# Order of work inside the last attention: head turning split in pairs around each projection, and the queries' projection one group earlier

## The reference, cut to what matters

```python
q = rms_norm(linear(x, q_w, q_b), norm_q_w).reshape(B, L, NH, HD)          # NH = 16 heads of HD = 32
k = rms_norm(linear(ctx_txt, k_w, k_b), norm_k_w).reshape(B, -1, NH, HD)    # text rows 257 to 360
v = linear(ctx_txt, v_w, v_b).reshape(B, -1, NH, HD)
k_img = rms_norm(linear(ctx_img, k_img_w, k_img_b), norm_k_img_w)...        # image rows 0 to 256
v_img = linear(ctx_img, v_img_w, v_img_b)...
img_x = attention(q, k_img, v_img)                                          # softmax over 257 rows
txt_x = attention(q, k, v)                                                  # softmax over 104 rows
out = (txt_x + img_x).reshape(B, L, DIM)
return linear(out, o_w, o_b)
```

## Time and profile before

| what | value |
|---|---|
| three executions | 2484.36, 2490.7, 2493.62 us; median 2490.7 us |
| span of the profiled execution | 2493.3 us |
| TensorE (PE) busy in the span | 2377.4 us, 95% |
| VectorE (DVE), ScalarE (ACT), GpSimd (POOL) busy | 54%, 32%, 29% |
| mean granted TensorE clock | 0.959 of full speed |
| last attention, from its first matmul to the next stage's | about 1936 to 2334 us |

### The profile page before, as it was taken

One profiled execution on the slowest core, in us unless ns is written; L12 is line 12 of the kernel. 1 busy time (PEld: TensorE's weight loads), 2 busy tenths in 40 slices (PEclk: granted clock), 3 DMA queues, 4 the chain that ended last, 5 costly groups with the idle time before them and its releaser, 6 DMA issues. The chain is left out here.

```text
span 2493.3 us, 30147 instructions
## 1 busy us (share of the span) xinstructions
PE 2377.4 (95%) x10329; PEld 1284.9 (52%) x10329; DVE 1345.9 (54%) x3448; ACT 786.8 (32%) x2069; POOL 733.4 (29%) x728
## 2 busy tenths in 40 slices
PE   8999999989999998999979999989999899999899
PEld 4455455656356555555555565544444344444454
DVE  5544344126111324667667767676664355555797
ACT  1134344303011113555541010231110255655433
POOL 3655455204100004321133433320000165665200
PEclk9999999999999998999959999889999899999799
DMA  6026200014275533110043222450000321111100
GB/s 193 1 80 227 79 17 8 0 52 135 89 286 207 202 133 87 49 38 30 1 154 129 92 76 101 164 195 6 4 9 5 110 59 46 55 47 29 37 13 15
DMA packets 93678, 203.31 MB, mean 82 GB/s; under 512 B 18580, under 2 KB 37428, under 8 KB 91864
## 3 DMA queue, kind: packets, MB, share of 16 engines
q1 hardware_dynamic: 87384, 188.26, 22.4%
q0 software_dynamic: 6144, 13.13, 1.9%
HBM read 150.45 MB, written 45.94 MB: 79 GB/s over the span
## 5 line engine op out<-in xcount | busy, mean ns | idle before, releaser
L3645 POOL TENSOR_SCALAR a_p<-a_p,a_li 100x257 f32<-100x257 f32 x252 | 188.0, 766 | 110.7 <-DVE a_li L3508 110.7
L633 POOL TENSOR_SCALAR a_shared<-a_shared,a_li 128x361 f32<-128x361 f32 x104 | 131.5, 1265 | 182.7 <-DVE a_li L541 182.7
L3263 PE MATMUL bank<-l_early,a_ctx 128*128 128x512 f32 (+1 forms) x384 | 180.1, 614 | 0.0
L2560 PE MATMUL bank<-s_xT,s_w 128*128 128x400 f32 x512 | 179.2, 504 | 0.8 <-PEq L2757 0.8
L2560 PEld LDWEIGHTS bank<-s_xT,s_w 128*128 128x128 f32 x512 | 98.2, 192 | 77.2 <-issue 4.1
L1853 POOL DMA_INDIRECT a_got<-slots_y,slots_of x32 | 33.7, 1054 | 318.6 <-POOLq L1193 309.8
L3263 PEld LDWEIGHTS bank<-l_early,a_ctx 128*128 128x128 f32 (+1 forms) x384 | 68.8, 188 | 85.0 <-issue 85.0
L313 PE MATMUL bank<-a_wk,a_ctx 128*128 128x512 f32 (+1 forms) x192 | 95.0, 616 | 9.3 <-DMA a_wk<-in_L_xattn_Wk 5.6
L691 ACT ACTIVATE a_shared<-a_shared,a_nm 128x361 f32<-128x361 f32 x104 | 62.1, 597 | 98.9 <-DVE a_nm L535 98.9
L2570 PE MATMUL bank<-f_h,s_w 128*128 128x400 f32 x256 | 90.9, 499 | 0.0
L2629 ACT ACTIVATE f_sg<-bank 128x400 f32<-128x400 f32 x32 | 16.1, 503 | 236.6 <-PE bank L2560 236.6
(11 more groups left out here) (477 smaller groups left out, 4985.1 us busy)
## 6 DMA issues: line engine op xcount, KB each, us to landing
slots_x<-zero SPq DMA_DIRECT2D x4, 4096.0 KB, 27.0
f_triple<-in_L_ffn_triples SPq DMA_DIRECT2D x16, 768.0 KB, 4.3
rounded<-f_triple SPq DMA_DIRECT2D x16, 768.0 KB, 3.3
s_whole<-in_L_ffn_w SPq DMA_DIRECT2D x24, 512.0 KB, 3.9
e_wg<-in_L_ffn_w_gate SPq DMA_DIRECT2D x16, 704.0 KB, 4.5
e_wu<-in_L_ffn_w_up SPq DMA_DIRECT2D x16, 704.0 KB, 6.1
e_wd<-in_L_ffn_w_down SPq DMA_DIRECT2D x16, 512.0 KB, 4.4
e_xg<-slots_x SPq DMA_DIRECT2D x16, 512.0 KB, 5.4
```

Source lines behind the costliest of these rows:

```text
L633: pool.tensor_scalar(p[s % NP], p[s % NP], li[:, b % 2, h:h + 1], None, ALU.mult).then_inc(normed, 1)
L2560: mm = nc.tensor.matmul(banks[f % 2][:, 0:GT], w[:, kc, f * P:(f + 1) * P], xT[:, kc, :], start=(kc == 0), stop=(kc == KC - 1))
L3263: mm = nc.tensor.matmul(bank[0:m, :], columns[:, kc], w[:, kc, :], start=(kc == 0), stop=(kc == KC - 1))
L3645: pool.tensor_scalar(p[g % 2][j][:, lo:hi], p[g % 2][j][:, lo:hi], li[:, h, i:i + 1], None, ALU.mult) \
```

## The change

In every pass of the loop (b = 0 to 6) each group now reads: scores, two heads turned, a product, two heads turned, the rest. `queries(n)` moves from the third group to the second; `values(n, 0)` from the second to the third; `values(n, 1)` goes behind `turn_keys` and `turn_queries`, which now come before `outputs(b, 2)`; `values(n, 2)` goes from before `scores(n, 0)` to behind them. The ring's list follows. On VectorE `copy_heads` is cut in pairs, the key scaling and `add_query_bias` move ahead of the third group's maxima, and in the last group the maxima and inverses of the next sequence's first group come before copies. On GpSimd `key_power` comes before `norm(b, 2)` instead of after it. ScalarE's order of squares, signs and copies follows.

```diff
@@ order of the ring
-            for g in range(G):
-                if more:
-                    order += [[("k", n, 0)], [("k", n, 2)], [("q", n)], [("v", n, 2)]][g]
-                elif g == 0:
-                    order += [("o", b - 1)]
-                order += [("t", b, GH * g + j) for j in range(GH)]
-                if more:
-                    order += [[("x", n), ("k", n, 1)], [("v", n, 0)],
-                              [("v", n, 1)] + [("kT", n, fb) for fb in range(KC)] + [("qT", n)], []][g]
-                if b > 0 and more and g == 3:
-                    order += [("o", b - 1)]
+            two = lambda g, i: [("t", b, GH * g + 2 * i + j) for j in range(2)]
+            if more:
+                order += two(0, 0) + [("k", n, 0)] + two(0, 1) + [("x", n), ("k", n, 1)]
+                order += two(1, 0) + [("k", n, 2)] + two(1, 1) + [("q", n)]
+                order += two(2, 0) + [("v", n, 0)] + two(2, 1) + [("kT", n, fb) for fb in range(KC)] + [("qT", n), ("v", n, 1)]
+                order += two(3, 0) + [("v", n, 2)] + two(3, 1) + ([("o", b - 1)] if b > 0 else [])
+            else:
+                order += [("o", b - 1)] + [("t", b, h) for h in range(NH)]
@@ TensorE
                     scores(b, 1)
+                    turn_heads(b, 0, (0, 1))
                     keys(n, 0)
-                    turn_heads(b, 0)
+                    turn_heads(b, 0, (2, 3))
                     turn_x(n)
                     keys(n, 1)
                     outputs(b, 0)
 
                     scores(b, 2)
+                    turn_heads(b, 1, (0, 1))
                     keys(n, 2)
-                    turn_heads(b, 1)
+                    turn_heads(b, 1, (2, 3))
+                    queries(n)
+                    outputs(b, 1)
+
+                    scores(b, 3)
+                    turn_heads(b, 2, (0, 1))
                     values(n, 0)
-                    outputs(b, 1)
-
-                    scores(b, 3)
-                    queries(n)
-                    turn_heads(b, 2)
+                    turn_heads(b, 2, (2, 3))
+                    turn_keys(n)
+                    turn_queries(n)
                     values(n, 1)
                     outputs(b, 2)
-                    turn_keys(n)
-                    turn_queries(n)
+
+                    scores(n, 0)
+                    turn_heads(b, 3, (0, 1))
                     values(n, 2)
-
-                    scores(n, 0)
-                    turn_heads(b, 3)
+                    turn_heads(b, 3, (2, 3))
                     if b > 0:
                         project_out(b - 1)
                     outputs(b, 3)
@@ VectorE
                     all_maxima(b, 1)
+                    copy_heads(b, 0, (0, 1))
                     add_bias(n, 0)
-                    copy_heads(b, 0)
+                    copy_heads(b, 0, (2, 3))
                     inverses(b, 1)
                     add_bias(n, 1)
 
                     all_maxima(b, 2)
+                    copy_heads(b, 1, (0, 1))
                     add_bias(n, 2)
-                    copy_heads(b, 1)
+                    lay_last_key(n)
+                    copy_heads(b, 1, (2, 3))
                     inverses(b, 2)
-                    lay_last_key(n)
+                    mean_key_squares(n)
                     if b + 2 < B:
                         measure(b + 2)
+                    scale_keys(n)
+                    add_query_bias(n)
 
                     all_maxima(b, 3)
-                    mean_key_squares(n)
-                    add_query_bias(n)
-                    copy_heads(b, 2)
+                    copy_heads(b, 2, (0, 1))
                     mean_query_squares(n)
-                    inverses(b, 3)
-                    scale_keys(n)
+                    copy_heads(b, 2, (2, 3))
                     scale_queries(n)
                     copy_keys(n)
-
-                    copy_heads(b, 3)
+                    inverses(b, 3)
+
                     all_maxima(n, 0)
+                    copy_heads(b, 3, (0, 1))
+                    inverses(n, 0)
+                    copy_heads(b, 3, (2, 3))
                     if b > 0:
                         add_output(b - 1)
-                    inverses(n, 0)
@@ GpSimd
                     norm(b, 1)
                     if b + 1 < B:
                         add_bias(b + 1)
+                        key_power(b + 1)
                     norm(b, 2)
                     if b + 1 < B:
-                        key_power(b + 1)
                         query_power(b + 1)
@@ ScalarE
                     exponentials(b, 2)
+                    squares(n, 2)
                     signs(b, 1)
-                    squares(n, 2)
+                    query_squares(n)
+
+                    exponentials(b, 3)
                     copy_values(n, 0)
-
-                    exponentials(b, 3)
-                    query_squares(n)
+                    copy_keys(n)
                     copy_values(n, 1)
-                    copy_keys(n)
-                    copy_values(n, 2)
                     if n == B - 1:
                         signs(b, 2)
+
                     exponentials(n, 0)
+                    copy_values(n, 2)
```

More of the change, by code:

```diff
@@ L3324, in scores, with turn_heads @@
                             .then_inc(scored, 1)
-                def turn_heads(b, g):
-                    for j in range(GH):
+                def turn_heads(b, g, heads=range(GH)):
+                    for j in heads:
                         h = GH * g + j
@@ L3389, in _ @@
                     scores(b, 2)
+                    turn_heads(b, 1, (0, 1))
                     keys(n, 2)
-                    turn_heads(b, 1)
-                    values(n, 0)
+                    turn_heads(b, 1, (2, 3))
+                    queries(n)
                     outputs(b, 1)
                     scores(b, 3)
-                    queries(n)
-                    turn_heads(b, 2)
+                    turn_heads(b, 2, (0, 1))
+                    values(n, 0)
+                    turn_heads(b, 2, (2, 3))
+                    turn_keys(n)
+                    turn_queries(n)
                     values(n, 1)
                     outputs(b, 2)
-                    turn_keys(n)
-                    turn_queries(n)
+                    scores(n, 0)
+                    turn_heads(b, 3, (0, 1))
                     values(n, 2)
-                    scores(n, 0)
-                    turn_heads(b, 3)
+                    turn_heads(b, 3, (2, 3))
                     if b > 0:
@@ L3530, in all_maxima, with copy_heads @@
                         maxima(b, g, j)
-                def copy_heads(b, g):
-                    for j in range(GH):
+                def copy_heads(b, g, heads=range(GH)):
+                    for j in heads:
                         copy_head(b, g, j)
```

## The result

| | before | after |
|---|---|---|
| median of the runs | 2490.86 us (5 runs) | 2475.31 us (5 runs, 2465.33 to 2476.90) |
| span of the profiled execution | 2493.3 us | 2466.6 us |
| last attention, first matmul to next stage | 398.43 us | 383.61 us |

The ratio is 0.993, 95% interval 0.991 to 0.9949: the change makes the kernel faster by 0.7%. I had forecast 0.9975 and "within 0.5%". The median lies just inside my range (2475 to 2495), on its lower edge, but the move, 0.7%, is nearly three times the 0.25% that I gave.

What follows compares the result with a forecast made beforehand. TensorE was taken to bound the kernel; steady passes -0.8, seam -2.5 and clock -3.0 us sum to -6.3, a span of 2487.0 us and a median of 2484.4 (ratio 0.9975), range 2475 to 2495 us.

Steps and rivals of the forecast that it cites:

- The place of the work: Last attention: TensorE sets the pace, work only moves, so a steady sequence can win only what TensorE loses in waits.
- the price list of the steady pass: TensorE's queue laid out step by step: remaining waits 1.45 us against 1.56, a sequence 44.12 us, -0.11.
- the 0.55 us wait that I put before `turn_queries`: Third group: `turn_queries` waits 0.55 us for VectorE's copy of the second key block, behind head copy and query scaling.
- The price of a pair of heads: Each group: six transpositions, two heads, priced at 0.76 us, half of 1.51.
- The clean price of a head: Kernel before: twelve transpositions with nothing in their way take 1.51 us, the measure for other groups' losses.
- the floor: Steady sequence at full clock without the counted waits: 44.23 - 1.56 = 42.67 us.
- all gone is -1.56: Bound for a steady sequence: with all six predicted waits gone, -1.56 us, or -10.9 us over seven passes.
- rival 1: The steady waits really go: 1.0 us a sequence won, -12.5 us in all, 2478 us; chance 0.20.
- The wait for `norm(b, 2)`: Third group's second head waits 0.40 us, as `norm(b, 2)` behind `key_power` starts 8.5 us after `scores(b, 2)`.
- The seam: Where sequence 0 gives way to 1: 11.56 us falls to 8.3, gain 3.2 us, net -2.5 us.
- The clock: Sequence 1: the low clock behind the idle stretch, costing a product 3.0 us more, no longer occurs: -3.0 us.
- rivals 2 and 4: Seam gains but clock still falls there: 2487.5 us, chance 0.12; clock falls in each sequence: 2505 us, chance 0.04.

Runs made afterwards that it cites:

- scores_forward: Changed kernel with the next group's scores before the bank-waiting step in groups 0, 1, 3, and `key_power` behind `norm(b, 2)`: steady pass 41.56 us, ratio 0.989.
- seam_only: Kernel before with the new order in the first pass (b = 0) only: seven passes 309.8 us against 316.9, ratio 0.9978.
- steady_only: Kernel before with the new order in passes b = 1 to 6 only: seven passes 309.7 us against 316.9, ratio 0.9978.
- root_behind_norm: Changed kernel with `key_power` put back behind `norm(b, 2)` on GpSimd: steady pass 49.4 to 51.1 us, ratio 1.0145 against the kernel before.
- inverses_early: Kernel before with `inverses(n, 0)` moved ahead of `add_output(b - 1)` on VectorE: steady pass 43.7 us against 44.23, ratio 0.9988.
- four_in_a_run: Changed kernel with pairs undone, each group turning four heads in one run behind its product: steady pass 44.6 us, ratio 0.9989 against the kernel before.

## Why the prediction was wrong

**The place of the work** was right: TensorE sets the pace, the product count is the same, and the gain lies in TensorE's waits, its clock and, for a smaller part that I hadn't foreseen, in shorter products. By starts, the 1.33 us of a steady pass are 0.77 in the turning of heads, 0.37 in the products and 0.19 before `scores(b, 1)`.

**The step that failed is the price list of the steady pass.** I gave a pass -0.11 us and it gained 1.33. The largest term of the miss is the 0.55 us wait that I put before `turn_queries`, and which isn't there (0.59 with what the turning itself took less). The price of a pair of heads was too high by more than the bank waits behind it were too low, which makes 0.28, and that of a product was too high, 0.29. Another 0.11 is a slip of the sum: my own prices and waits add up to 44.01 us, and I wrote 44.12. The rest, outputs and scores, is 0.05 the other way.

**The clean price of a head** came from the first step, the floor. I wrote that "a run of twelve transpositions with nothing in their way takes 1.51 us (2159.01 to 2160.52)". It had something in its way. TensorE's weight loads in the kernel before at that place:

```profile
2159.01 0.85 PEld L3336 LDWEIGHTS bank<-ident,a_p 100*128 100x128 f32 x9 [0.53 <-issue]
2160.11 0.32 PEld L3336 LDWEIGHTS bank<-ident,a_p 100*128 100x128 f32 x3 [0.26 <-issue]
```

Nine loads, three heads, in 0.85 us, and then a gap before the fourth head. VectorE in the kernel before at that time:

```profile
2159.53 1.60 DVE L3513 COPY a_pt<-bank 128x300 f32<-128x300 f32 x4 [4.60 <-PE bank L3336]
```

The first of these copies lasts 0.47 us, so the first head's bank is free at 2160.0, and the fourth head, three places later in a ring of three banks, starts at 2160.11. `norm` of that group had ended at 2155.98, so it isn't that. The timeline of the matmuls hides this, since their modelled ends reach over the gap, and no idle time is written. Nine loads of 0.15 us each in 0.85 start 0.087 apart. A pair of heads with its neighbours is 0.59 us in the changed kernel, and two more heads at that distance add 0.52, so I estimate a run of four without any wait at 1.11 and not 1.51. The third group's run in the kernel before, which I had not read from its starts:

```profile
2146.69 0.69 PE L3336 MATMUL bank<-ident,a_p 100*128 100x100 f32 x6
...
2148.46 3.70 PE L3263 MATMUL bank<-l_early,a_ctx 128*128 128x512 f32 x8
```

It takes 1.77 us. The four runs of a pass of before therefore lost not 1.4 us but 7.47 - 4.44 = 3.0 (2.48, 1.71, 1.77 and 1.51), and my bound "all gone is -1.56" was no bound: scores_forward takes 2.67 us from the pass.

**The sizes in the new order**, by my own terms. First pairs: 4 x 0.76 + 0.40 predicted, 3 x 0.59 + 0.80 = 2.57 measured, -0.87. Second pairs with the waits behind them: 3.54 predicted, 1.13 + 1.03 + 1.04 + 0.93 = 4.13 measured, +0.59: against a clean pair of 0.59 to 0.62, a late bank is worth 0.3 to 0.5 us, not 0.05 to 0.20, as the clean pair is shorter and TensorE reaches the bank earlier. Together -0.28. Products: 8 x 3.55 = 28.40 predicted, 28.11 measured, -0.29; a product behind a first pair is 3.44 to 3.46 from start to start, and why it is 0.08 shorter there than behind scores no run shows. Key and query turning: 1.94 + 0.55 predicted, 1.90 measured, -0.59. With the two kinds of pairs taken together, this is the largest single miss. VectorE's timeline of the changed kernel:

```profile
2083.37 0.84 DVE L3514 COPY a_pt<-bank 128x300 f32<-128x300 f32 x2 [1.31 <-PE bank L3333]
2084.13 0.74 DVE L3493 SCALAR_TENSOR_TENSOR a_q<-a_q,a_qr,a_nq 100x512 f32<-100x512 f32 x1
2084.79 0.53 DVE L3498 COPY a_kT<-bank 128x361 f32<-128x361 f32 x1
```

The scaling starts 1.23 us behind the start of the pair (2082.90), where I had the last head's copy done at 1.42. It takes 0.74, not the 0.96 that it took beside `norm`; here GpSimd has nothing to do from 2082.71 to 2086.26. And `turn_keys` starts 1.04 behind its pair, 0.2 later than I had it. So the block's copy begins 0.85 behind `turn_keys`, as early as before (0.88), ends at 2085.32, and `turn_queries` at 2085.47 doesn't wait for it. My rival 1 named just this, that the two waits priced highest "rest on short differences of long sums". Its time, 2478, came closest, and I gave it 0.20. That was in part luck: of its two waits one went and the other stayed, at half its price; the rest of the pass's gain is the prices above.

**The wait for `norm(b, 2)`** came as written, at 0.21 instead of 0.40: GpSimd starts it 8.18 us behind `scores(b, 2)` (2075.93), where I had 8.5. This `norm` ran beside `scale_keys` and took 6.00 us for four heads, against 5.76 for the three others of the pass; the whole 0.24 us is in one of its eight instructions, 1.17 us instead of 0.94. The Trainium skill ("GPSIMD Engine Reference", section "Specifications") says that GpSimd shares its SBUF interfaces with VectorE and contends with VectorE instructions that have two SBUF inputs. The trace agrees, and the size is small.

**The seam** was right in kind, and its gross price low: 3.8 us for 3.2.

**The clock** was right: no fall before the last sequence, 3.0 us, and seam_only with steady_only show that it hangs on the seam. The Trainium skill ("TensorE: Matmul & The Clock Gate", section "What's actually happening") has the low clock as the default, lifted by activity; the traces agree. root_behind_norm shows it once more: a wait of 5.1 us, then a product at 6.47 us. In the last sequence, whose queue isn't touched, the clock falls some 9 us behind `scores(7, 1)` in both kernels. In the changed kernel that is at 2281 us, so it lies ahead of the 2290 that I had named as the end of the stretch to watch; it doesn't speak for rivals 2 and 4.

**The sum.** Predicted: steady passes -0.8, seam -2.5, clock -3.0. Measured over the seven passes: seam and clock together 7.1 - 1.3 = 5.8, when one pass's steady gain is taken off seam_only, against 5.5; the remaining 8.4 are the steady part, against 0.8. So nearly the whole miss is in the steady passes. Of the 1.33 us a pass, 0.5 is the first group's late `norm` (inverses_early), 0.5 the pairs, 0.35 the products' places with what came along; that is the split in this order of steps, and four_in_a_run shows that another order would give another. That a wait for the first head's bank caused the 0.26 us gap in the kernel before is read from starts and was not tried by itself; four_in_a_run shows a wait of that kind written out, 0.37 us.

## What to carry to other kernels

Before a stretch is taken as the clean price of an operation, look at its single starts or at the engine's loads: matmuls with modelled ends covered here a gap of a quarter of a microsecond in which no idle time is written. In a ring of a few banks, count for each step who had its bank last and how long that reader takes; with three banks, a fourth quick step in a row waited for the first one's reader, and cutting the run around a long product took it from 1.71 to 1.53 us with the wait behind it. A wait for a bank can be filled with any work that needs no bank of the ring, here the scores, which was worth another 10.9 us of the stage. Split a long sum of small prices into its terms afterwards and check that they add up to what was written: here the slip alone was as large as the predicted gain of a pass. And an uncovered stretch, as at the seam of the first two passes, cost twice: the wait, and the low clock behind it.

## What the hardware showed that I hadn't expected

An idle stretch of 5.1 us in each pass, once every 50 us, was enough for a product mostly at the low clock each time (4.96 to 6.60 us for 3.46), although TensorE had no wait of over 0.5 us in the rest of a steady pass. At the old seam, two waits of under 0.7 us and eight matmuls spaced 0.4 us apart were enough. And code that did not change, ahead of the stage, took 12.2 us more in one execution than in another, with a clock of 0.96 and 0.97: on this kernel that is nearly as much as the whole change, so single spans can't be compared.
